# Attention over eight images: low-part products in groups of eight steps, V and q/k in other places

## The chip, the cores and the metric

The program runs on one core of a Trainium2 chip. The metric is the device time in microseconds of one execution. The engines are PE (TensorE, matmuls), DVE (VectorE), ACT (ScalarE), POOL (GpSimd) and SP (SyncE, which here only issues transfers). All times below are in microseconds unless marked otherwise.

## The reference

Self-attention over 8 images with 128 channels and 1024 pixels, with 64 channels for q and k; softmax runs over the second pixel index, and the result is scaled by gamma and added to the input.

```python
q = jnp.einsum('oc,bcn->bon', Wq, xf) + bq[None, :, None]
k = jnp.einsum('oc,bcn->bon', Wk, xf) + bk[None, :, None]
v = jnp.einsum('oc,bcn->bon', Wv, xf) + bv[None, :, None]
attn = jnp.einsum('bci,bcj->bij', q, k)
attn = jax.nn.softmax(attn, axis=-1)
out = jnp.einsum('bcn,bmn->bcm', v, attn).reshape(b, c, h, w)
return gamma * out + x
```

## The kernel before

An image is worked in two chunks of 512 pixels i (the queries), a chunk in 8 steps of 128 pixels j (the keys): 16 steps for an image, 128 in all. fp32 products are made from rounded high parts and low parts. The work of step s is a loop over s on each engine, written out by hand; semaphores couple them, and nothing but this order and the semaphores decides when something runs.

What PE does in step s, in this order:

- `score_tile(s + 2)` (L537, L538): the scores of the step after next, transposed, into one of two banks. It waits until ACT has read the bank two steps before (`weight_hi_done`).
- `max_jobs(s)` (L495, "mx" below): from step 18 on one product of 128 queries with 512 keys into a bank of `work`, from which DVE takes the row maximum (L768) that the softmax of a later chunk subtracts. In the first 18 steps a table, `EARLY_MAXES`, says how many, up to two.
- `sums_hi(s - 2)` (L556): four matmuls of 258 columns that add the high parts of the weights times the values to `sums`. Those of a chunk's first step wait, at the first and the third matmul, until DVE has read the sums of the chunk before (`sums_freed`).
- every `BURST` steps `sums_lo` (L572), the burst: the bf16 low parts of the weights of those steps times `values_b`. Of 16 matmuls (4 steps by 4 tiles) before. It goes through the first half of the tiles and then the second; after a chunk's last step each half releases `sums_done`.
- `side_jobs(s)`: with k the step in the image, V's product (L489, eight fp32 passes) in k = 1 and 9, the transposed output (L505) in k = 6 and 14, q and k together of the image after next (L482 to L484) in k = 7 and 11.

The mx products and the side jobs share the two banks of `work` in turn: job n takes the bank of job n - 2 and waits in `take_bank` until that has been read out. q/k is read out by ACT (`qk_hi`, L671) and then DVE (`qk_lo`, L759), V by ACT (L682) and then DVE (L764), an mx by DVE alone.

ACT makes, for the scores two steps ahead, two exponentials (L704 fp32 `weight`, L707 rounded `weight_hi`), then copies the low sums after a chunk's last step (`take_low_sum`, L713), then the side job, and in k = 3 and 5 the rounded input `x_hi` (L678). DVE makes in iteration s the side job of step s - 1, the maxima of step s, in steps k = 4, 8, 13, 15 and 0 of the weights their low part (`weight_lo`, L809, one iteration ahead), and behind a chunk's last step the total (L817) and its reciprocal. POOL makes the other low parts (L419), the scaled output (L426) in k = 3 and 11, `x_lo` (L400) in k = 4 and 6, and `values_b` (`short_values`, L411) in k = 2 and 10. `weight`, `weight_hi` and `weight_lo` are rings of 8 steps.

Of the kernel before, what the change touches and what calls it, by code (L numbers as in the profile page):

```python
# [5 lines left out]
BATCHES = 8  # L6
CHANNELS = 128
HEAD = 64
PIXELS = 32 * 32
TILE = 128  # L10
CHUNK = 512
# [8 lines left out]
VCOLS = 2 * CHANNELS + 2  # L20
# [3 lines left out]
RING = 8  # L24
# [12 lines left out]
ALL_ON_POOL = 8  # L37


BURST = 4  # L40

SPREAD_MX, SPREAD_REST = 4, 2

EARLY = 18
EARLY_MAXES = {5: (2, 0, 1), 6: (2, 1, 2), 7: (2, 3, 1), 8: (2, 4, 2), 9: (2, 6, 1), 10: (2, 7, 1),
               11: (3, 0, 1), 12: (3, 1, 2), 13: (3, 3, 1), 14: (3, 4, 1), 15: (3, 5, 1), 16: (3, 6, 1), 17: (3, 7, 1)}


def max_jobs(s):
# [3 lines left out]
    if s < EARLY:  # L55
        c, first, count = EARLY_MAXES.get(s, (0, 0, 0))
        return [(c, i) for i in range(first, first + count)]
# [4 lines left out]
def side_jobs(s):  # L62

    b, k = divmod(s, STEPS)
    jobs = []
    if k == 1 and b > 0:
        jobs.append(("v", b, 1))
    if b == 0 and k == 4:
        jobs.append(("mt", 1, 0))
    if k == 6 and b > 0:  # L70
        jobs.append(("out", 2 * b - 1, 0))
    if k in (7, 11) and b + 2 < BATCHES:
        jobs.append(("qk", b + 2, (7, 11).index(k)))
    if k == 9 and b + 1 < BATCHES:
        jobs.append(("v", b + 1, 0))
    if k == 14:
        jobs.append(("out", 2 * b, 0))
    return jobs


# [15 lines left out]
def low_on_dve(s):  # L96
    return s >= ALL_ON_POOL and s % STEPS in DVE_LOW
# [16 lines left out]
def loads(n, each=1):  # L114
    return 16 * each * ((n + 1) // 2 if n % 2 else n // 2)
# [7 lines left out]
def attention_program(nc, x, Wq, bq, Wk, bk, Wv, bv, gamma, out):  # L123
    fp32 = mybir.dt.float32
    fp32r = mybir.dt.float32r
    bf16 = mybir.dt.bfloat16
    ALU = mybir.AluOpType
# [6 lines left out]
    with ExitStack() as ctx:  # L134
        def sbuf(name, shape, dtype):
            return ctx.enter_context(nc.sbuf_tensor(name, shape, dtype))

        def psum(name, shape, dtype):
            return ctx.enter_context(nc.psum_tensor(name, shape, dtype))

        def sem(name):
            return ctx.enter_context(nc.semaphore(name))
# [34 lines left out]

        weight = sbuf("weight", [TILE, RING, CHUNK], fp32)
        weight_hi = sbuf("weight_hi", [TILE, RING, CHUNK], fp32r)
        weight_lo = sbuf("weight_lo", [TILE, RING, CHUNK], bf16)  # L180

        low_sum = sbuf("low_sum", [TILE, CHUNK_TILES, CHANNELS + 1], fp32)
        total = sbuf("total", [TILE, CHUNK_TILES, CHANNELS + 1], fp32)
# [5 lines left out]
        sums = psum("sums", [TILE, CHUNK_TILES, CHUNK], fp32)  # L189
# [18 lines left out]
        weight_lo_pool_done = sem("weight_lo_pool_done")  # L208
# [34 lines left out]
        weight_lo_done = sem("weight_lo_done")  # L243
# [13 lines left out]
        def tile(t):  # L257
            return slice(t * TILE, (t + 1) * TILE)
# [10 lines left out]
        def quarter(half):  # L269
            return slice(half * CHUNK_TILES, (half + 1) * CHUNK_TILES)  # L270
# [23 lines left out]
        def wait_lo_summed(engine, s):  # L294

            if s >= 0 and s % TILES >= TILES - BURST:
                engine.wait_ge(sums_done, 2 * (s // TILES + 1))
            elif s >= 0:
                engine.wait_ge(burst_done, s // TILES + 1)
# [66 lines left out]
        def _(pool):  # L366
# [42 lines left out]
            def short_values(n, half):  # L409
                pool.wait_ge(v_hi_done, HALVES * n + half + 1)  # L410
                pool.tensor_scalar(values_b[n % 2][:, quarter(half), 0:CHANNELS],  # L411
                                   values[n % 2][:, quarter(half), CHANNELS:2 * CHANNELS].bitcast(fp32), 0.0, 1.0,
                                   ALU.add, ALU.mult).then_inc(values_b_done, 1)

            def low_weights(s):
                pool.wait_ge(weight_hi_done, s + 1)
                wait_lo_summed(pool, s - RING)
                r = s % RING
                pool.tensor_tensor(weight_lo[:, r], weight[:, r], weight_hi[:, r], ALU.subtract).then_inc(weight_lo_pool_done, 1)  # L419

            def scale(c):
                pool.wait_ge(one_over_done, c + 1)

                wait(pool, out_turned, c)
                by = one_over[:, :].rearrange("p (t a) -> p t a", a=1).broadcast_to([TILE, CHUNK_TILES, CHANNELS])
                pool.tensor_tensor(scaled[:, :], total[:, :, 0:CHANNELS], by, ALU.mult).then_inc(scaled_done, 1)  # L426
# [10 lines left out]
            for s in range(ALL_STEPS):  # L437
                b, k = divmod(s, STEPS)
                if s + 1 < ALL_STEPS and not low_on_dve(s + 1):
                    low_weights(s + 1)  # L440
                if k == 3 and b > 0:
                    scale(2 * b - 1)
                if k == 11:
                    scale(2 * b)
                if k == 2 and b > 0:
                    short_values(b, 1)
                if k in (4, 6) and b + 2 < BATCHES:
                    rest_of_x(b + 2, (4, 6).index(k))
                if k == 10 and b + 1 < BATCHES:
                    short_values(b + 1, 0)  # L450

        @block.tensor
        def _(pe):
# [54 lines left out]
            def do_max(c, i):  # L508
                n, h = divmod(c, HALVES)
                if n > 0 and h == 0 and i == 0:  # L510
                    pe.wait_ge(spread_mx[n % 2], loads(n, SPREAD_MX))
                max_scores(n, h * CHUNK_TILES + i // 2, i % 2, take_bank(("mx", c, i)))

            def do_job(job):
                name, n, i = job
                place = take_bank(job)
                if name == "qk":
                    project_qk(n, i, place)
                elif name == "v":
                    wait_x(pe, n)  # L520
                    project_v(n, i, place)
                elif name == "mt":
                    pe.wait_ge(neg_max_r_done, n + 1)
                    turn_max(n, place)
                elif name == "out":
                    pe.wait_ge(scaled_done, n + 1)
                    turn_out(range(CHUNK_TILES), place)
# [32 lines left out]
            def sums_lo(s):  # L560

                b, k = divmod(s, STEPS)
                h, p = k // TILES, b % 2
                steps = range(s - BURST + 1, s + 1)
                if h == 0:
                    pe.wait_ge(values_b_done, HALVES * b + (k % TILES) // CHUNK_TILES + 1)
                for i in steps:
                    wait_low(pe, i)

                def lo(it, i):  # L570
                    j = i % TILES
                    return pe.matmul(sums[:, it, CHANNELS:VCOLS], weight_lo[:, i % RING, tile(it)],  # L572
                                     values_b[p][:, j], start=False, stop=(j == TILES - 1))

                for half in range(2):
                    for it in tiles_of_half(half):
                        for i in steps:
                            last = lo(it, i)
                    if s % TILES == TILES - 1:
                        last.then_inc(sums_done, 1)  # L580
                    elif half == 1:
                        last.then_inc(burst_done, 1)
# [50 lines left out]
            for s in range(ALL_STEPS + LAG):  # L633
                if s + AHEAD < ALL_STEPS:
                    score_tile(s + AHEAD)
                if s < ALL_STEPS:
                    for c, i in max_jobs(s):
                        do_max(c, i)
                if s >= LAG:
                    if s == LAG:  # L640

                        pe.wait_ge(qk_lo_done, HALVES)
                        pe.wait_ge(max_rows_done, 1)
                    sums_hi(s - LAG)
                    if (s - LAG) % BURST == BURST - 1:
                        sums_lo(s - LAG)
                if s < ALL_STEPS:
                    for job in side_jobs(s):
                        do_job(job)

            for half in range(2):
                pe.wait_ge(last_scaled, half + 1)
# [103 lines left out]
        def _(dve):  # L756
# [39 lines left out]
            def do_job(job):  # L796
                name, n, i = job
                if name == "qk":
                    rest_of_qk(n, i, bank(bank_of(job)))
                elif name == "v":  # L800
                    rest_of_v(n, i, bank(bank_of(job)))
                elif name == "out":
                    finish(n, bank(bank_of(job)))

            def low_weights(s):
                r = s % RING
                dve.wait_ge(weight_hi_done, s + 1)
                wait_lo_summed(dve, s - RING)
                dve.tensor_tensor(weight_lo[:, r], weight[:, r], weight_hi[:, r], ALU.subtract).then_inc(weight_lo_done, 1)  # L809

            def add_half(c, half):
                its = tiles_slice(half)
# [46 lines left out]
            for s in range(ALL_STEPS):  # L859
                b, k = divmod(s, STEPS)  # L860
# [55 lines left out]
```

## Time and profile before

| what | us |
|---|---|
| median of 3 runs | 240.57 |
| lowest and highest | 240.35, 241.44 |
| the profiled execution | 241.74 |
| its span in the trace | 239.7 |
| PE busy | 229.3 (96%) |
| ACT busy | 179.6 (75%) |
| POOL busy | 174.6 (73%) |
| DVE busy | 169.5 (71%) |

The profile records every instruction on each engine. A matmul is drawn until its modelled end, which overlaps the next one's start; so what PE's work takes is read from start to start. A timeline row merges instructions of one group that follow each other; its first two numbers are the start and the length, and a bracket at its end gives the idle time before it and the engine that ended it.

### The profile page before, as it was taken

What the parts mean: (1) busy time and instruction counts of PE and PEld (TensorE: products, weight loads), DVE (VectorE), ACT (ScalarE), POOL (GpSimd) and SP (SyncE); (2) the same over time, 40 slices, a digit from 0 to 9 for tenths busy, and PEclk for the clock granted to TensorE, in tenths of its full rate; (3) what the DMA queues carried; (4) which work ended last, traced back from release to release, by engine and by line L of the source; (5) the groups of instructions that cost most, each with busy time, mean ns of one, the idle gap of its engine ahead of it and who ended that gap; (6) DMA issues with size and microseconds to landing.
All of it is one profiled execution on the core that took longest, in us unless ns stands there. A gap on an engine that the chain in (4) does not pass through costs nothing.

```text
span 239.7 us, 4848 instructions
## 1 busy us (share of the span) xinstructions
PE 229.3 (96%) x1676; PEld 196.8 (82%) x1676; DVE 169.5 (71%) x287; ACT 179.6 (75%) x345; POOL 174.6 (73%) x158
## 2 busy tenths in 40 slices
PE   7997989899999999999999999999999999999992
PEld 7364968798889988898888898898888899899890
DVE  1486396776869768786869768787769767683354
ACT  2769768579786878779876887788776868778840
POOL 8568996279963898568972898658982977679750
PEclk9999999999999999999999999999999999999996
DMA  3714700490408403390407504291106601010101
GB/s 91 230 51 103 162 0 1 80 229 6 131 0 198 111 26 110 69 236 4 131 4 177 131 3 133 40 233 38 44 3 151 158 0 45 4 44 3 44 37 51
DMA packets 16103, 19.86 MB, mean 83 GB/s; under 512 B 9808, under 2 KB 10320, under 8 KB 16080
## 3 DMA queue, kind: packets, MB, share of 16 engines
q1 hardware_dynamic: 15840, 19.54, 33.0%
q8 instruction: 13, 0.21, 0.4%
q14 instruction: 10, 0.08, 0.1%
q10 hardware_dynamic: 240, 0.03, 0.1%
HBM read 4.33 MB, written 4.19 MB: 36 GB/s over the span
## 4 chain that ended last, share of the span: by engine, by line
PE 92%; DVE 3%; ACT 3%; issue 1%; POOL 0%; POOLq 0%; DVEq 0%
PE sums L556 25%; PE sums L572 13%; PE scores L537 12%; PE work L495 12%; PE scores L538 12%; PE work L489 6%; PE work L505 3%; PE sums L586 2%; PE work L483 1%; PE work L484 1%; PE work L482 1%; DVE neg_max L768 1%; DVE qk_lo L759 1%; PE scores L489 1%; PE sums L478 1%
## 5 line engine op out<-in xcount | busy, mean ns | idle before, releaser
L419 POOL TENSOR_TENSOR weight_lo<-weight,weight_hi 128x512 bf16<-128x512 f32 x90 | 122.5, 1381 | 43.6 <-ACT weight_hi L707 43.4
L768 DVE TENSOR_REDUCE neg_max<-work 128x1 f32<-128x512 f32 x120 | 81.8, 686 | 22.9 <-PE work L495 22.4
L704 ACT ACTIVATE weight<-scores 128x512 f32<-128x512 f32 x128 | 76.9, 600 | 27.5 <-PE scores L538 24.7
L556 PEld LDWEIGHTS sums<-values,weight_hi 128*128 128x128 f32 x512 | 78.1, 188 | 10.2 <-issue 0.5
L556 PE MATMUL sums<-values,weight_hi 128*128 128x258 f32 x512 | 81.7, 282 | 0.1
L707 ACT ACTIVATE weight_hi<-scores 128x512 fp32r<-128x512 f32 x128 | 76.9, 600 | 0.0
L537 PE MATMUL scores<-q_hihi,k_hilo 128*128 128x512 f32 x128 | 54.5, 426 | 1.1 <-ACT weight_hi L707 1.1
L495 PE MATMUL work<-k_hilo,q_hihi 128*128 128x512 f32 x120 | 48.9, 413 | 2.4 <-DVE qk_lo L759 2.0
L538 PE MATMUL scores<-q_lomax,k_hione 128*128 128x512 f32 x128 | 50.4, 393 | 0.0
L809 DVE TENSOR_TENSOR weight_lo<-weight,weight_hi 128x512 bf16<-128x512 f32 x38 | 36.5, 961 | 2.7 <-ACT weight_hi L707 2.7
L572 PE MATMUL sums<-values_b,weight_lo 128*128 128x130 bf16 x512 | 35.5, 221 | 0.0
L495 PEld LDWEIGHTS work<-k_hilo,q_hihi 128*128 128x128 f32 x120 | 22.4, 188 | 14.5 <-DVE qk_lo L759 6.5
L572 PEld LDWEIGHTS sums<-values_b,weight_lo 128*128 128x128 bf16 x512 | 29.8, 98 | 1.5
L537 PEld LDWEIGHTS scores<-q_hihi,k_hilo 128*128 128x128 f32 x128 | 24.2, 189 | 3.2 <-ACT weight_hi L707 1.9
L538 PEld LDWEIGHTS scores<-q_lomax,k_hione 128*128 128x128 f32 x128 | 24.3, 190 | 0.6
L817 DVE TENSOR_TENSOR total<-sums,low_sum 128x258 f32<-128x258 f32 x32 | 13.6, 427 | 11.7 <-ACT low_sum L713 11.1
L713 ACT ACTIVATE low_sum<-sums 128x256 f32<-128x256 f32 x32 | 12.4, 386 | 6.9 <-PE sums L572 4.7
L426 POOL TENSOR_TENSOR scaled<-total,one_over 128x512 f32<-128x512 f32 x15 | 15.6, 1042 | 0.0
L489 PE MATMUL work<-w_v_t,x_sb 128*128 128x128 f32 x112 | 15.5, 281 | 0.0
L400 POOL TENSOR_TENSOR x_lo<-x_sb,x_hi 128x512 fp32r<-128x512 f32 x12 | 15.4, 1284 | 0.0
L411 POOL TENSOR_SCALAR values_b<-values 128x512 bf16<-128x512 f32 x16 | 9.9, 617 | 7.1 <-ACT values L682 7.1
L764 DVE TENSOR_TENSOR values<-work,values 128x512 fp32r<-128x512 f32 x14 | 9.7, 692 | 7.3 <-ACT values L682 7.3
(78 smaller groups left out, 167.6 us busy)
## 6 DMA issues: line engine op xcount, KB each, us to landing
out<-y_sb SPq DMA_DIRECT2D x15, 256.0 KB, 2.4
x_sb<-in_x SPq DMA_DIRECT2D x7, 512.0 KB, 4.0
q_hihi<-qk_hi SPq DMA_DIRECT2D x14, 256.0 KB, 3.8
k_hilo<-qk_hi SPq DMA_DIRECT2D x7, 256.0 KB, 3.1
k_hilo<-qk_lo SPq DMA_DIRECT2D x7, 256.0 KB, 4.9
q_lomax<-qk_lo SPq DMA_DIRECT2D x7, 256.0 KB, 5.0
k_hione<-qk_hi SPq DMA_DIRECT2D x7, 256.0 KB, 4.9
q_lomax<-neg_max_r SPq DMA_DIRECT2D x56, 0.5 KB, 2.1
```

Source lines behind the costliest of these rows:

```text
L419: pool.tensor_tensor(weight_lo[:, r], weight[:, r], weight_hi[:, r], ALU.subtract).then_inc(weight_lo_pool_done, 1)
L426: pool.tensor_tensor(scaled[:, :], total[:, :, 0:CHANNELS], by, ALU.mult).then_inc(scaled_done, 1)
L489: last = pe.matmul(place[:, tile(t)], image(n)[:, tile(half * CHUNK_TILES + t)], w_v_t[:, :], start=True, stop=True)
L495: pe.matmul(place, q_hihi[p][:, tile(t)], k_hilo[p][:, chunk(h)], start=True, stop=True).then_inc(mx_done, 1)
L537: pe.matmul(scores[:, s % 2], k_hilo[p][:, tile(j)], q_hihi[p][:, chunk(h)], start=True, stop=False)
L538: pe.matmul(scores[:, s % 2], k_hione[p][:, tile(j)], q_lomax[p][:, chunk(h)], start=False, stop=True).then_inc(scores_done, 1)
L556: last = pe.matmul(sums[:, it, 0:VCOLS], weight_hi[:, r, tile(it)], values[p][:, j], start=(j == 0), stop=False)
L572: return pe.matmul(sums[:, it, CHANNELS:VCOLS], weight_lo[:, i % RING, tile(it)], values_b[p][:, j], start=False, stop=(j == TILES - 1))
L704: act.activation(weight[:, r], scores[:, s % 2], ACT.Exp)
L707: act.activation(weight_hi[:, r], scores[:, s % 2], ACT.Exp).then_inc(weight_hi_done, 1)
L768: dve.reduce_max(neg_max[:, t, h:h + 1], place, AX.X, negate=True).then_inc(neg_max_done, 1)
L809: dve.tensor_tensor(weight_lo[:, r], weight[:, r], weight_hi[:, r], ALU.subtract).then_inc(weight_lo_done, 1)
```

## The change

- `BURST` is 8 instead of 4: a burst holds 32 matmuls (8 steps by 4 tiles) and comes once for each chunk, in k = 1 and k = 9, no more in k = 5 and 13. `weight_lo` becomes a ring of 16 steps (`LOW_RING`).
- V's two halves are made in k = 15 of the image before and in k = 3, not in k = 9 of the image before and k = 1. On POOL `short_values` moves to k = 0 and k = 4.
- q/k is made in k = 8 and 12, and on PE ahead of `sums_hi` of that step; the other side jobs stay behind it.
- Four entries of `EARLY_MAXES` change, so that the steps of the first image with a q/k product hold one mx, and steps 7 and 11 hold two.

```diff
-BURST = 4
+BURST = 8
+LOW_RING = 16
...
-EARLY_MAXES = {5: (2, 0, 1), 6: (2, 1, 2), 7: (2, 3, 1), 8: (2, 4, 2), 9: (2, 6, 1), 10: (2, 7, 1),
+EARLY_MAXES = {5: (2, 0, 1), 6: (2, 1, 2), 7: (2, 3, 2), 8: (2, 5, 1), 9: (2, 6, 1), 10: (2, 7, 1),
...
-    if k == 1 and b > 0:
+    if k == 3 and b > 0:
         jobs.append(("v", b, 1))
...
-    if k in (7, 11) and b + 2 < BATCHES:
-        jobs.append(("qk", b + 2, (7, 11).index(k)))
-    if k == 9 and b + 1 < BATCHES:
-        jobs.append(("v", b + 1, 0))
+    if k in (8, 12) and b + 2 < BATCHES:
+        jobs.append(("qk", b + 2, (8, 12).index(k)))
     if k == 14:
         jobs.append(("out", 2 * b, 0))
+    if k == 15 and b + 1 < BATCHES:
+        jobs.append(("v", b + 1, 0))
...
-                wait_lo_summed(pool, s - RING)
+                wait_lo_summed(pool, s - LOW_RING)
...
-                if k == 2 and b > 0:
+                if k == 0 and b > 0:
+                    short_values(b, 0)
+                if k == 4 and b > 0:
                     short_values(b, 1)
                 if k in (4, 6) and b + 2 < BATCHES:
                     rest_of_x(b + 2, (4, 6).index(k))
-                if k == 10 and b + 1 < BATCHES:
-                    short_values(b + 1, 0)
...
+                    for job in side_jobs(s):
+                        if job[0] == "qk":
+                            do_job(job)
                 if s >= LAG:
...
                     for job in side_jobs(s):
-                        do_job(job)
+                        if job[0] != "qk":
+                            do_job(job)
```

On PE, around the end of an image (step k = 1 of the next one): the sums and the burst that end a chunk, and what follows up to the first sums of the new chunk. Before:

```order
L556 MATMUL sums<-values1,weight_hi 128x258 x4
L572 MATMUL sums<-values_b1,weight_lo 128x130 x16
L489 MATMUL work<-w_v_t,x_sb 128x128 x4
L537 MATMUL scores<-q_hihi0,k_hilo0 128x512
L538 MATMUL scores<-q_lomax0,k_hione0 128x512
L495 MATMUL work<-k_hilo1,q_hihi1 128x512
L556 MATMUL sums<-values0,weight_hi 128x258 x4
```

And of the change:

```order
L557 MATMUL sums<-values1,weight_hi 128x258 x4
L573 MATMUL sums<-values_b1,weight_lo 128x130 x32
L538 MATMUL scores<-q_hihi0,k_hilo0 128x512
L539 MATMUL scores<-q_lomax0,k_hione0 128x512
L496 MATMUL work<-k_hilo1,q_hihi1 128x512
L557 MATMUL sums<-values0,weight_hi 128x258 x4
```

The burst is twice as long, and V's product no longer stands between it and the new chunk's sums.

On DVE, around steps 7 to 9 of an image: the output's last addition, the maxima, a low part of the weights and the low part of q/k. Before:

```order
L786 SCALAR_TENSOR_TENSOR y_sb<-work,gamma_bv,x_sb 128x512
L768 TENSOR_REDUCE neg_max<-work 128x1
L809 TENSOR_TENSOR weight_lo<-weight,weight_hi 128x512
L759 SCALAR_TENSOR_TENSOR qk_lo<-work,b_qk,qk_hi 128x512
L768 TENSOR_REDUCE neg_max<-work 128x1 x2
```

And of the change:

```order
L791 SCALAR_TENSOR_TENSOR y_sb<-work,gamma_bv,x_sb 128x512
L773 TENSOR_REDUCE neg_max<-work 128x1
L814 TENSOR_TENSOR weight_lo<-weight,weight_hi 128x512
L773 TENSOR_REDUCE neg_max<-work 128x1
L764 SCALAR_TENSOR_TENSOR qk_lo<-work,b_qk,qk_hi 128x512
L773 TENSOR_REDUCE neg_max<-work 128x1
```

A maximum stands directly behind the low part now, with qk_lo one place later.

On POOL, in steps 4 to 8 of an image: low parts of the weights and the two x_lo. Before:

```order
L419 TENSOR_TENSOR weight_lo<-weight,weight_hi 128x512
L400 TENSOR_TENSOR x_lo<-x_sb,x_hi 128x512
L419 TENSOR_TENSOR weight_lo<-weight,weight_hi 128x512 x2
L400 TENSOR_TENSOR x_lo<-x_sb,x_hi 128x512
L419 TENSOR_TENSOR weight_lo<-weight,weight_hi 128x512 x3
```

And of the change:

```order
L420 TENSOR_TENSOR weight_lo<-weight,weight_hi 128x512
L412 TENSOR_SCALAR values_b<-values 128x4x128
L401 TENSOR_TENSOR x_lo<-x_sb,x_hi 128x512
L420 TENSOR_TENSOR weight_lo<-weight,weight_hi 128x512 x2
L401 TENSOR_TENSOR x_lo<-x_sb,x_hi 128x512
```

values_b stands in this chain now, ahead of the first x_lo.

## Rows read from the trace of the kernel before

**Rows 1.** Windows: busy time of each engine (instructions), clock, DMA share, GB/s.

```profile
105.00:118.00 13.00, 13.00 (x102) 11.65 (x101) 9.50 (x17) 10.77 (x22) 12.24 (x11) 1.00 0.35 82
```

**Rows 2.** Timeline of PE, image 3, steps 1 to 6: start, length, group.

```profile
105.74 1.11 PE L572 MATMUL sums<-values_b,weight_lo 128*128 128x130 bf16 x16
106.69 1.11 PE L489 MATMUL work<-w_v_t,x_sb 128*128 128x128 f32 x8
107.55 0.48 PE L537 MATMUL scores<-q_hihi,k_hilo 128*128 128x512 f32 x1
107.86 0.40 PE L538 MATMUL scores<-q_lomax,k_hione 128*128 128x512 f32 x1
...
108.80 0.40 PE L537 MATMUL scores<-q_hihi,k_hilo 128*128 128x512 f32 x1
...
112.35 1.11 PE L572 MATMUL sums<-values_b,weight_lo 128*128 128x130 bf16 x16
113.27 0.48 PE L537 MATMUL scores<-q_hihi,k_hilo 128*128 128x512 f32 x1
```

**Rows 3.** Timeline of PE in the opening: V without a burst before it.

```profile
14.35 1.05 PE L489 MATMUL scores<-w_v_t,x_sb 128*128 128x128 f32 x8
15.16 0.71 PE L495 MATMUL work<-k_hilo,q_hihi 128*128 128x512 f32 x2
```

**Rows 4.** Timeline of PE, image 3, step 9.

```profile
118.24 0.39 PE L538 MATMUL scores<-q_lomax,k_hione 128*128 128x512 f32 x1
118.55 0.50 PE L495 MATMUL work<-k_hilo,q_hihi 128*128 128x512 f32 x1
118.89 0.65 PE L556 MATMUL sums<-values,weight_hi 128*128 128x258 f32 x4
```

**Rows 5.** PE in image 0: a wait of step 12 in the timeline; both waits summed.

```profile
43.00 0.50 PE L495 MATMUL work<-k_hilo,q_hihi 128*128 128x512 f32 x1 [0.89 <-DVE qk_lo L759]
43.34 0.63 PE L556 MATMUL sums<-values,weight_hi 128*128 128x258 f32 x4
...
PE work L495 <- DVE qk_lo L759: 2.0, 2, 1.2
```

**Rows 6.** Timeline of ACT and DVE behind the burst of 105.74.

```profile
106.42 0.85 ACT L713 ACTIVATE low_sum<-sums 128x256 f32<-128x256 f32 x2
106.83 0.90 DVE L817 TENSOR_TENSOR total<-sums,low_sum 128x258 f32<-128x258 f32 x2 [0.49 <-ACT low_sum L713]
```

**Rows 7.** Timeline of PE in the last image, behind the burst of step 9.

```profile
225.37 0.40 PE L538 MATMUL scores<-q_lomax,k_hione 128*128 128x512 f32 x1
...
225.88 0.80 PE L556 MATMUL sums<-values,weight_hi 128*128 128x258 f32 x4
```

**Rows 8.** Timeline of ACT in image 3, V and the exponential behind it.

```profile
107.83 0.60 ACT L682 ACTIVATE values<-work 128x512 fp32r<-128x512 f32 x1 [0.56 <-PE work L489]
108.33 0.59 ACT L704 ACTIVATE weight<-scores 128x512 f32<-128x512 f32 x1
```

**Rows 9.** Timeline of DVE and POOL, image 3, steps 2 to 8, and the tail.

```profile
108.52 0.62 POOL L411 TENSOR_SCALAR values_b<-values 128x512 bf16<-128x512 f32 x1 [0.27 <-ACT values L682]
...
110.63 1.56 POOL L419 TENSOR_TENSOR weight_lo<-weight,weight_hi 128x512 bf16<-128x512 f32 x1 [0.49 <-ACT weight_hi L707]
...
112.15 1.28 POOL L400 TENSOR_TENSOR x_lo<-x_sb,x_hi 128x512 fp32r<-128x512 f32 x1
...
113.37 2.56 POOL L419 TENSOR_TENSOR weight_lo<-weight,weight_hi 128x512 bf16<-128x512 f32 x2
...
115.87 1.32 POOL L400 TENSOR_TENSOR x_lo<-x_sb,x_hi 128x512 fp32r<-128x512 f32 x1
...
116.47 1.27 DVE L809 TENSOR_TENSOR weight_lo<-weight,weight_hi 128x512 bf16<-128x512 f32 x1
...
228.21 1.04 POOL L426 TENSOR_TENSOR scaled<-total,one_over 128x512 f32<-128x512 f32 x1
...
228.31 1.48 DVE L809 TENSOR_TENSOR weight_lo<-weight,weight_hi 128x512 bf16<-128x512 f32 x1 [1.98 <-ACT weight_hi L707]
```

More of the change, by code:

```diff
@@ L37 @@
 ALL_ON_POOL = 8
-BURST = 4
+BURST = 8
+LOW_RING = 16
 SPREAD_MX, SPREAD_REST = 4, 2
 EARLY = 18
-EARLY_MAXES = {5: (2, 0, 1), 6: (2, 1, 2), 7: (2, 3, 1), 8: (2, 4, 2), 9: (2, 6, 1), 10: (2, 7, 1),
-               11: (3, 0, 1), 12: (3, 1, 2), 13: (3, 3, 1), 14: (3, 4, 1), 15: (3, 5, 1), 16: (3, 6, 1), 17: (3, 7, 1)}
+EARLY_MAXES = {5: (2, 0, 1), 6: (2, 1, 2), 7: (2, 3, 2), 8: (2, 5, 1), 9: (2, 6, 1), 10: (2, 7, 1),
+               11: (3, 0, 2), 12: (3, 2, 1), 13: (3, 3, 1), 14: (3, 4, 1), 15: (3, 5, 1), 16: (3, 6, 1), 17: (3, 7, 1)}
 def max_jobs(s):
@@ L179, in attention_program @@
         weight_hi = sbuf("weight_hi", [TILE, RING, CHUNK], fp32r)
-        weight_lo = sbuf("weight_lo", [TILE, RING, CHUNK], bf16)
+        weight_lo = sbuf("weight_lo", [TILE, LOW_RING, CHUNK], bf16)
         low_sum = sbuf("low_sum", [TILE, CHUNK_TILES, CHANNELS + 1], fp32)
@@ L416, in low_weights @@
                 pool.wait_ge(weight_hi_done, s + 1)
-                wait_lo_summed(pool, s - RING)
+                wait_lo_summed(pool, s - LOW_RING)
                 r = s % RING
-                pool.tensor_tensor(weight_lo[:, r], weight[:, r], weight_hi[:, r], ALU.subtract).then_inc(weight_lo_pool_done, 1)
+                pool.tensor_tensor(weight_lo[:, s % LOW_RING], weight[:, r], weight_hi[:, r], ALU.subtract).then_inc(weight_lo_pool_done, 1)
             def scale(c):
@@ L571, in lo @@
                     j = i % TILES
-                    return pe.matmul(sums[:, it, CHANNELS:VCOLS], weight_lo[:, i % RING, tile(it)],
+                    return pe.matmul(sums[:, it, CHANNELS:VCOLS], weight_lo[:, i % LOW_RING, tile(it)],
                                      values_b[p][:, j], start=False, stop=(j == TILES - 1))
@@ L807, in low_weights @@
                 dve.wait_ge(weight_hi_done, s + 1)
-                wait_lo_summed(dve, s - RING)
-                dve.tensor_tensor(weight_lo[:, r], weight[:, r], weight_hi[:, r], ALU.subtract).then_inc(weight_lo_done, 1)
+                wait_lo_summed(dve, s - LOW_RING)
+                dve.tensor_tensor(weight_lo[:, s % LOW_RING], weight[:, r], weight_hi[:, r], ALU.subtract).then_inc(weight_lo_done, 1)
             def add_half(c, half):
```

## The prediction

> **What bounds the kernel now.** I read a thirteen-microsecond window of the steady part first: TensorE (PE) is busy all of it, DVE 9.5, ACT 10.8 and POOL 12.2, at a granted clock of 1.00, the 2.4 GHz level [rows 1]. So a microsecond counts only where PE loses it, and busy time does not say where that is, because a matmul that waits for its weights is drawn longer. I therefore read the distances between the starts of PE's groups. In a step without extras, scores take 0.23 + 0.23, the maxima's product (L495, "mx") 0.235 and the four sums 0.48: 1.18. I call Tn the start of the scores issued in step n of an image, so T2 is 107.55 and T3 108.80 [rows 2]; image b has steps 0 to 15, and PE never stands still except where a distance exceeds these. Two kinds of losses are visible: waits for a bank of `work` behind q and k, and a longer first score after every other kind of matmul. The profiled run is 241.74 for a span of 239.7; the median shown is 240.57. I sum changes of the span and add them to the median.
>
> **1. Waits behind q and k: gone, gain 4.0.** The mx two jobs after a q/k product needs its bank, and gets it after ACT's qk_hi and DVE's qk_lo. In step 9 this makes two distances 0.31 and 0.34 instead of 0.235 [rows 4]: 0.2 lost, the same in step 13, in images 1 to 5: 5 × 0.4 = 2.0. In image 0, whose steps 8 and 12 hold two mx, the waits are 1.16 and 0.89 [rows 5]; counted by starts 0.26 more each (a matmul drawn 0.39 long against a distance of 0.235, and 0.10 for the late weights): 1.4 + 1.15 = 2.6. In the new order q and k stand ahead of the sums, 0.48 earlier before that mx, and the q/k of step 8 also has the burst of 32 behind it. It asks for the bank 0.48 later where it asked 0.2 too early, so this wait goes with 0.28 to spare, if ACT and DVE are as prompt. In image 0 DVE now meets five mx in steps 5 to 7 without the burst between: at 0.69 each against two mx per 1.4, I let it give back 0.3 in step 7 and 0.3 in step 12. Net 2.0 + 2.6 − 0.6 = 4.0.
>
> **2. Fewer switches: gain 0.7.** A burst of 16 alone takes 0.92 and its first score afterwards 0.31 instead of 0.23; burst and V together 0.95 + 0.86 + the same 0.08 [rows 2]. The change halves the bursts, but takes V away from them, so that V pays a return of its own: six returns per image before and six after. What is left: V alone took 0.81 in the opening instead of 0.86 [rows 3], and a burst of 32 should take 0.01 + 32 × 0.0589 − 0.03 = 1.87 (0.0589 is what 16 pitches make of 0.95, less the first's 0.01). Per image 2 × (0.99 + 1.89) = 5.76 becomes 2 × (1.95 + 0.89) = 5.68. Eight images: 0.7. Were all halved bursts worth a return, it would be 2 × 0.08 × 8 = 1.3; the least is zero.
>
> **3. The end of each chunk loses its cover: loss 3.3.** This is the term that the diff doesn't show. Before a new chunk's sums may overwrite `sums`, ACT copies the low sum and DVE adds, by halves (`sums_freed`). In the old burst this is over 1.99 after its start (106.83 + 0.90 = 107.73, burst at 105.74), that is 1.10 after its last matmul began [rows 6]. V, 0.86 on PE, lay over it. Now the last of 32 begins 1.84 into the burst; the second half is free at 2.94, PE hears of it at 3.00. PE, with no V, reaches the third of the next sums' matmuls at 1.87 + 0.31 + 2 × 0.235 + 2 × 0.118 = 2.89. A matmul whose weights come late begins some 0.105 after that load (43.00 to 43.34, where 0.235 is the rule [rows 5]), so it starts at 3.11: 0.22 lost. The old trace has one chunk end without V, in the last image, also without mx: there 538 takes 0.51 instead of 0.23, and the four sums are drawn 0.80 long instead of 0.64, a loss of 0.28 + 0.16 = 0.44 [rows 7]; with an mx of 0.235 ahead, 0.21 is what the sum gives. Thirteen chunk ends in images 0 to 6 at 0.22 are 2.9; that of step 1 in the last image has no mx and costs 0.45; that of step 9 there is unchanged. 3.3. The least it can be is 0 (if I mistake the order of readers), the most 15 × 0.44 = 6.6.
>
> **4. V in step 3 delays ACT: loss 0.3.** ACT starts V 0.03 after V's matmuls end (107.83 [rows 8], V drawn from 106.69 for 1.11 [rows 2]), so at T3 + 2.27, and follows with x_hi, both ahead of the exponentials of step 6's weights. Operations of 0.6 follow each other there after 0.50 [rows 8]: with V, x_hi and the first exponential at 0.5 each and the second at 0.6, ACT is done at T3 + 4.37, and score 8 wants it at T3 + 4.47. With 0.06 for the signal and 0.105 for late weights, 0.06 is lost in images 1 to 5. Zero to 0.15 each.
>
> **5. DVE's low part of step 8 against POOL's second x_lo: loss 3.3, or nothing.** DVE and POOL hold each other up here: DVE's weight_lo takes 0.68 alone, but 1.27 when issued at 116.47 into POOL's x_lo of 115.87, and 1.48 at 228.31, one tenth behind POOL's product of 228.21 [rows 9]. The reverse is seen too: POOL's weight_lo of 110.63 takes 1.56 instead of 1.28. Before, the q/k of step 7 and not step 8's mx was next on DVE, and nothing of PE waited. Now mx 9 takes the bank of mx 8, and DVE reads mx 8 right behind this weight_lo. When does it start? POOL begins weight_lo 5 at T3 + 1.83 (110.63 − 108.80); 1.47 later short_values (now here; 0.62 drawn, 0.58 counted), x_lo (112.15 to 113.37: 1.23), two low parts (113.37 to 115.87: 2.50) and then the second x_lo at T3 + 7.61. DVE's low part stands at T7 + 1.6, as before. T7 is T3 + 1.18 + 0.81 (V) + 1.26 + 1.22 + 0.06 (4.) + 1.53 (step 6 with out) = T3 + 6.06; DVE is there at T3 + 7.66, five hundredths behind POOL. If that counts as behind, the low part ends 0.6 after x_lo, at T3 + 9.5; mx 8 is read at 10.2, and mx 9, due on PE at T9 + 0.47 = T3 + 9.67, starts at 10.34: 0.67 lost, in each of images 1 to 5: 3.3. The bounds are 0 and, with image 0, 4.0. I take the loss: rows at one tenth behind show the block in full, and anything more that delays PE between steps 3 and 7 keeps DVE behind for up to another 1.2, while POOL's chain has little to delay it.
> The Trainium skill has a rule on this ("SBUF — State Buffer", section "SBUF: two separate sides"): a DVE operation with two SBUF inputs and a GpSimd operation that reads SBUF exclude each other, and whichever starts first has the port pair for its whole instruction. By that rule the sum is the one with the loss; without it, it would be 3.3 less. The trace agrees with full blocking (1.48 for 0.68), and has no row within five hundredths.
>
> **What costs nothing.** The ring of 16 removes no wait, since waits on freed low parts don't show in the trace. DVE's part of V in step 15 ends just under 0.1 before mx needs the bank, as after V now. The next image's spread is issued about as late as before, because it also waits for the last scores. In the tail both orders do the same matmuls after the last exponential: −0.1, with 0.1 lost in the last image's steps without mx, where PE no longer leaves ACT a burst to catch up.
>
> **Sum.** −4.0 − 0.7 + 3.3 + 0.3 + 3.3 = +2.2 to 2.4 (2.35 before rounding): 240.57 + 2.35 = **242.9**.
>
> **Rivals.** (A) DVE gets ahead of POOL in step 7. For it: five hundredths is within the error of a sum of nine distances. Then 3.35 is not lost: −1.0, 239.6 (238.8 to 240.6). (B) The forecast, slower: 242.9 (242 to 244); it decides from the point at which DVE's low part starts after x_lo. (C) The cover of 3. isn't needed, because ACT or DVE is faster behind a longer burst than behind a short one, and A holds too: −1.0 − 3.0 gives 236.6. Against it stands the last image's row. (D) The race is lost a second time: DVE's low part of the next step 0 starts 0.08 ahead of POOL's (it does so now); behind it, V's rest on DVE ends at T1 + 1.1 instead of 0.35, and the mx of step 1, due at 0.47, waits some 0.65 in seven images: 242.9 + 4.5 = 247.4. (E) Some images block and some don't: 240 to 242.
>
> **How the numbers follow.** B 0.45, A 0.27, C 0.10, D 0.08, E 0.10. The range 238.8 to 244.2 leaves out C, D and a rim of A. A measurement tells about 0.5% from no change, that is 239.4 to 241.8. Faster: C and 0.12 of A, 0.22. The same: the rest of A and most of E, 0.25. Slower: B, D, a little E: 0.53. B's own range is 242.0 to 244.2.
>
> **What would show it.** The sums of steps 2 and 10 at 0.70 instead of 0.48 (3.); 538 and mx of steps 10 and 14 at 0.235 (1.); V at 0.81 and the burst at 1.87 (2.); a weight_lo of 1.8 on DVE in step 7 or 8 and an mx of step 9 that waits for neg_max (5.; in A it is 0.68 and no wait); score 8 waiting for weight_hi (4.). The prediction is wrong if the sums behind a burst of 32 don't wait, or if DVE slips in ahead of x_lo.

## The result, and the profile after

The changed kernel takes 245.2 us (median of 4, 244.6 to 245.5) beside 240.8 for the kernel before: 1.018 times as long, 95% interval 1.015 to 1.021, which is 4.3 us more (3.5 to 5.0). The forecast was 242.9, with 244.2 as the upper end.

PE's busy share and clock say nothing of this. The page and the same window as in [rows 1]:

```profile
PE 232.1 (96%) x1676; PEld 197.9 (82%) x1676; DVE 166.2 (68%) x287; ACT 180.2 (74%) x345; POOL 175.5 (72%) x158
...
PE 84%; DVE 9%; ACT 4%; issue 2%; POOL 0%; POOLq 0%; DVEq 0%
...
105.00:118.00 13.00, 12.85 (x96) 11.03 (x93) 9.43 (x16) 10.57 (x22) 10.87 (x10) 1.00 0.32 84
```

The second line is the chain that ended last. In the kernel before it was PE for 92% and DVE for 3%; now DVE holds 9% of it. The waits, summed over the whole span of the changed kernel (engine, operation, who ended the wait: us, times, longest; PEld is PE's loading of weights), name the places:

```profile
PEld work L496 <- DVE neg_max L773: 5.9, 10, 0.7
PEld sums L557 <- DVE total L822: 2.8, 15, 0.4
PEld work L490 <- DVE y_sb L791: 1.2, 7, 0.2
```

None of the three is in the list of before, except a neg_max wait of 1.4 in all; the wait for qk_lo, 6.5 in all there, is gone. What they are in the steady part is read from PE's starts, as before. Image 3 of the changed kernel, the chunk end of step 1 (timeline):

```profile
104.69 2.04 PE L573 MATMUL sums<-values_b,weight_lo 128*128 128x130 bf16 x32
105.83 0.39 ACT L718 ACTIVATE low_sum<-sums 128x256 f32<-128x256 f32 x1 [0.62 <-PE sums L573]
106.25 0.43 DVE L822 TENSOR_TENSOR total<-sums,low_sum 128x258 f32<-128x258 f32 x1 [0.96 <-ACT low_sum L718]
106.53 0.48 PE L538 MATMUL scores<-q_hihi,k_hilo 128*128 128x512 f32 x1
106.76 0.38 ACT L718 ACTIVATE low_sum<-sums 128x256 f32<-128x256 f32 x1 [0.55 <-PE sums L573]
107.18 0.43 DVE L822 TENSOR_TENSOR total<-sums,low_sum 128x258 f32<-128x258 f32 x1 [0.50 <-ACT low_sum L718]
107.32 0.85 PE L557 MATMUL sums<-values,weight_hi 128*128 128x258 f32 x4
...
108.01 0.39 PE L538 MATMUL scores<-q_hihi,k_hilo 128*128 128x512 f32 x1
```

The four sums take 0.69 (107.32 to 108.01) instead of 0.48: the second half's total ends at 107.61, 2.92 after the burst began, and their third matmul waits for it. In [rows 6] the same two additions were over 1.99 after the burst, with V still on PE.

Steps 8 and 9 of the same image:

```profile
115.64 1.30 POOL L401 TENSOR_TENSOR x_lo<-x_sb,x_hi 128x512 fp32r<-128x512 f32 x1
115.68 1.80 DVE L814 TENSOR_TENSOR weight_lo<-weight,weight_hi 128x512 bf16<-128x512 f32 x1
...
117.41 0.68 DVE L773 TENSOR_REDUCE neg_max<-work 128x1 f32<-128x512 f32 x1
117.45 0.40 PE L539 MATMUL scores<-q_lomax,k_hione 128*128 128x512 f32 x1
...
118.14 0.50 PE L496 MATMUL work<-k_hilo,q_hihi 128*128 128x512 f32 x1 [0.30 <-DVE neg_max L773]
118.49 0.64 PE L557 MATMUL sums<-values,weight_hi 128*128 128x258 f32 x4
```

DVE's low part starts 0.04 after POOL's x_lo (0.07 in the next image) and takes 1.80 instead of 0.68. The maximum behind it, which reads the bank that the mx of step 9 takes, is over at 118.09, and that mx, whose two distances were 0.31 and 0.34 in [rows 4], has 0.69 and 0.35: 0.57 lost against 0.235 twice.

Behind q and k the mx of step 10 comes without a wait, and the sums behind it wait as those of step 2 do:

```profile
121.13 0.40 PE L539 MATMUL scores<-q_lomax,k_hione 128*128 128x512 f32 x1
121.37 0.40 PE L496 MATMUL work<-k_hilo,q_hihi 128*128 128x512 f32 x1
121.60 0.85 PE L557 MATMUL sums<-values,weight_hi 128*128 128x258 f32 x4
122.29 0.39 PE L538 MATMUL scores<-q_hihi,k_hilo 128*128 128x512 f32 x1
```

Step 15, V behind the output:

```profile
128.62 0.75 DVE L791 SCALAR_TENSOR_TENSOR y_sb<-work,gamma_bv,x_sb 128x512 f32<-128x512 f32 x1
128.82 0.63 PE L557 MATMUL sums<-values,weight_hi 128*128 128x258 f32 x4
...
129.42 1.16 PE L490 MATMUL work<-w_v_t,x_sb 128*128 128x128 f32 x8
...
130.34 0.48 PE L538 MATMUL scores<-q_hihi,k_hilo 128*128 128x512 f32 x1
```

V is due 0.48 after the sums and starts after 0.60, then takes 0.92 instead of the 0.81 of [rows 3]: 0.22 lost, because its bank holds the output, which DVE adds up until 129.37.

Most useful is the length of an image, from the start of the scores issued in step 0 to the same place of the next, since the opening ahead of it differs by up to 1.3 us between these profiles (that start stands at 19.7 in the profile of before and 18.7 in that of the change). From the timelines:

| kernel | image 0 | each of images 1 to 5 | image 6 |
|---|---|---|---|
| before | 29.10 | 27.3 | 25.50 |
| the change | 27.23 | 28.13 | 26.08 |
| e1_xlo_later | 27.69 | 27.58 | 26.11 |
| e8_v_in_step_0 | (30.22) | 27.84 | 25.83 |
| e7_pool_nudge | (33.35) | 27.57 | 26.09 |
| e6_second_v_back | 27.24 | 27.61 | 25.87 |
| e10_both_waits | 26.67 | 27.30 | 25.80 |
| e3_qk_only | 27.16 | 26.93 | 25.54 |
| e4_burst_only | 28.46 | 27.97 | 25.38 |
| e2_v_back | 27.33 | 26.79 | 25.40 |
| e9_v_back_short_start | 26.50 | 26.79 | 25.40 |

With bursts of 32, image 0 holds 16 low matmuls fewer (0.95) and the last image as many more. The two values in brackets are of executions with a long wait in image 0 that comes and goes (its rows stand in the last section); the ratios leave out the long executions: two of the four of e7_pool_nudge (247.8, 248.5) and one each of e8_v_in_step_0 (246.5), e5_v_back_short_ends (240.6) and e6_second_v_back (245.8, not profiled). Between the change and before, images 0 to 6 differ by −1.87 + 4.13 + 0.58, and the rest of the span, from step 0 of the last image, by 30.02 − 28.90 = 1.12: 3.96 together. The whole spans differ by 3.0 only, because the profiled execution of before had the longer opening.

### The profile page after: what moved, and what is told of

It is laid out like the page before. It is cut to its first block, busy times and chain, and to the rows that moved or that the text cites. A ratio compares the mean times of both kernels' runs of the same rounds, so it can differ in the third digit from the quotient of the medians.

```text
span 242.7 us, 4840 instructions
## 1 busy us (share of the span) xinstructions
PE 232.1 (96%) x1676; PEld 197.9 (82%) x1676; DVE 166.2 (68%) x287; ACT 180.2 (74%) x345; POOL 175.5 (72%) x158
## 4 chain that ended last, share of the span: by engine, by line
PE 84%; DVE 9%; ACT 4%; issue 2%; POOL 0%; POOLq 0%; DVEq 0%
PE sums L557 24%; PE sums L573 12%; PE work L496 11%; PE scores L538 11%; PE scores L539 10%; PE work L490 6%; DVE weight_lo L814 4%; PE work L506 3%; DVE neg_max L773 2%; PE sums L587 2%; DVE y_sb L791 1%; PE scores L490 1%; PE work L483 1%; PE sums L479 1%; ACT weight L709 1%
## 5 line engine op out<-in xcount | busy, mean ns | idle before, releaser
L420 POOL TENSOR_TENSOR weight_lo<-weight,weight_hi 128x512 bf16<-128x512 f32 x90 | 124.1, 1397 | 45.3 <-ACT weight_hi L712 45.3
L557 PEld LDWEIGHTS sums<-values,weight_hi 128*128 128x128 f32 x512 | 79.1, 188 | 12.8 <-DVE total L822 2.8
L557 PE MATMUL sums<-values,weight_hi 128*128 128x258 f32 x512 | 84.6, 285 | 0.4 <-DVE total L822 0.4
L496 PE MATMUL work<-k_hilo,q_hihi 128*128 128x512 f32 x120 | 48.3, 409 | 1.9 <-DVE neg_max L773 1.8
L814 DVE TENSOR_TENSOR weight_lo<-weight,weight_hi 128x512 bf16<-128x512 f32 x38 | 34.0, 894 | 3.0 <-ACT weight_hi L712 3.0
L573 PE MATMUL sums<-values_b,weight_lo 128*128 128x130 bf16 x512 | 32.7, 220 | 0.0
L687 ACT ACTIVATE values<-work 128x512 fp32r<-128x512 f32 x14 | 8.4, 600 | 8.6 <-PE work L490 8.6
```

What stands on the lines that cost most here:

```text
L420: pool.tensor_tensor(weight_lo[:, s % LOW_RING], weight[:, r], weight_hi[:, r], ALU.subtract).then_inc(weight_lo_pool_done, 1)
L496: pe.matmul(place, q_hihi[p][:, tile(t)], k_hilo[p][:, chunk(h)], start=True, stop=True).then_inc(mx_done, 1)
L557: last = pe.matmul(sums[:, it, 0:VCOLS], weight_hi[:, r, tile(it)], values[p][:, j], start=(j == 0), stop=False)
L814: dve.tensor_tensor(weight_lo[:, s % LOW_RING], weight[:, r], weight_hi[:, r], ALU.subtract).then_inc(weight_lo_done, 1)
```

## The experiments

### The port: e1_xlo_later

```diff
-                if k in (4, 6) and b + 2 < BATCHES:
-                    rest_of_x(b + 2, (4, 6).index(k))
+                if k in (4, 8) and b + 2 < BATCHES:
+                    rest_of_x(b + 2, (4, 8).index(k))
```

> The changed kernel with one number changed: POOL makes the second x_lo of an image in its iteration 8 instead of 6, so that it doesn't stand in the way of DVE's low part of step 8. Theory of the port race: the low part takes 0.7 instead of 1.80, the mx of step 9 comes without a wait (538 at 0.23 instead of 0.69), 0.57 less in each of images 1 to 5, 2.9 in all: some 242.3 us beside 245.2. Rival (mx 9 waits because qk_hi and qk_lo come late, whatever POOL does): no change, 245.

242.25 us, 1.007 times the kernel before (1.0045 to 1.009), where the change has 1.018: 2.6 us came back by the ratios, 2.9 were expected. An image takes 27.58 instead of 28.13; image 0 is 0.46 longer in this profile, where DVE's low part of its step 8 takes 1.83 instead of 1.36. DVE's low part in its timeline, and PE's step 9:

```profile
116.12 0.68 DVE L814 TENSOR_TENSOR weight_lo<-weight,weight_hi 128x512 bf16<-128x512 f32 x1
...
117.89 0.40 PE L539 MATMUL scores<-q_lomax,k_hione 128*128 128x512 f32 x1
118.12 0.40 PE L496 MATMUL work<-k_hilo,q_hihi 128*128 128x512 f32 x1
```

0.68 and 0.23: no wait. q/k is where it was, so the rival on qk_lo falls.

### The port again, by added work: e7_pool_nudge

```diff
+                if k == 5 and b + 2 < BATCHES:
+                    pool.memset(scratch[:, :], 0.0)
```

(`scratch` is a new tile that nothing else uses.)

> The changed kernel with one operation more: POOL sets 128x128 elements of an unused tile to zero in its iteration 5, some 0.2 us, so that its second x_lo starts some 0.15 behind DVE's low part of step 8 instead of 0.04 before it (115.64 and 115.68 in the changed kernel). Theory of the port race: the added work makes the kernel faster, the low part takes 0.7, the mx of step 9 comes without a wait, 5 times 0.57 less: 242.4 us beside 245.2. Rival (POOL's load as such, or qk_lo, delays step 9): unchanged or slower, 245.2 to 246.2.

1.010 times the kernel before (1.007 to 1.013), some 242.9 us, where the change has 1.018. An image takes 27.57, as in e1_xlo_later. The added 0.2 us on POOL reverses who starts first:

```profile
148.00 0.69 DVE L817 TENSOR_TENSOR weight_lo<-weight,weight_hi 128x512 bf16<-128x512 f32 x1
148.10 1.75 POOL L402 TENSOR_TENSOR x_lo<-x_sb,x_hi 128x512 fp32r<-128x512 f32 x1
```

Now POOL's x_lo is the one held up (1.75 for 1.3), and nobody waits for that. The rule of the Trainium skill ("SBUF — State Buffer", section "SBUF: two separate sides"), that whichever of the two starts first keeps the port for its whole instruction, agrees with these traces down to a lead of 0.04 us one way (the change) and 0.10 the other (here).

### V behind the bursts again: e2_v_back

```diff
-    if k == 3 and b > 0:
+    if k == 1 and b > 0:
         jobs.append(("v", b, 1))
...
-    if k == 15 and b + 1 < BATCHES:
+    if k == 9 and b + 1 < BATCHES:
         jobs.append(("v", b + 1, 0))
```

(with POOL's `short_values` back in k = 2 and 10)

> The changed kernel with V's halves (and POOL's short_values) back where they were before: behind the bursts of steps 9 and 1. Theory: V covers the reading of the sums again, so the sums behind a chunk's end take 0.48 instead of 0.69 (13 times 0.22 and once 0.45, 3.3 us), the wait of V in step 15 for the bank of the output goes (7 times 0.22, 1.5 us), and POOL's second x_lo starts earlier than DVE's low part needs the way, which takes the 2.9 us of step 9 as well: some 238 us. Rival (the longer burst of 32 costs by itself, by starving ACT and DVE): V's place gives back 3.3 at most, 242 us.

237.3 us, 0.986 times the kernel before (0.983 to 0.988), 7.9 us less than the change. Its chunk end in step 1:

```profile
103.85 1.11 PE L490 MATMUL work<-w_v_t,x_sb 128*128 128x128 f32 x8
104.71 0.48 PE L538 MATMUL scores<-q_hihi,k_hilo 128*128 128x512 f32 x1
...
105.50 0.64 PE L557 MATMUL sums<-values,weight_hi 128*128 128x258 f32 x4
105.98 0.39 PE L538 MATMUL scores<-q_hihi,k_hilo 128*128 128x512 f32 x1
```

The sums take 0.48 behind the same burst of 32. So its length is not what makes them wait; V's place is. In this kernel DVE's low part of step 8 takes 1.01, and step 9 has no wait. What the long burst is worth in total is told behind e4_burst_only.

### One half of V back: e6_second_v_back

```diff
-    if k == 3 and b > 0:
+    if k == 1 and b > 0:
         jobs.append(("v", b, 1))
```

> The changed kernel with only V's second half back behind the burst of step 1; the first half stays in step 15. Theory of the lost cover: the sums of step 2 take 0.48 again, those of step 10 still 0.69; 6 times 0.22 and once 0.45, 1.8 us. PE is also 0.9 earlier in step 7 while POOL's chain stays, so DVE's low part falls into POOL's low part before x_lo and waits less, and most of the 2.9 us of step 9 goes too: 241 us. Rival (the sums behind a burst wait because of its length, not because V is missing): step 2 stays at 0.69, and only the race changes: 242.5 us.

241.6 us, 1.0045 times the kernel before (1.002 to 1.007). The two chunk ends of one image separate the theories: in image 4 the sums of step 2 go from 134.72 to 135.20, 0.48, those of step 10 from 147.59 to 148.28, 0.69. But only 0.2 of step 9's 0.57 went, not most of it: DVE's low part, at 141.86, falls into POOL's low part ahead of x_lo and still takes 1.62. An image is 0.52 shorter: 0.22 at the chunk end, 0.2 in step 9, 0.12 for steps 5 and 6, where ACT no longer makes V and x_hi in a row, less 0.04 for V's own reading.

### V's first half in step 0: e8_v_in_step_0

```diff
+    if k == 0 and b > 0:
+        jobs.append(("v", b, 0))
...
-    if k == 15 and b + 1 < BATCHES:
-        jobs.append(("v", b + 1, 0))
```

> The changed kernel with V's first half in step 0 of its own image instead of step 15 of the one before. Theory: in step 15 V waits for the bank of the transposed output of step 14, which DVE reads late (7 times 0.22); in step 0 the bank is free, and the burst of step 1 covers V's reading (0.05 less too). The port race is left as it is. 245.2 - 1.9 = 243.3 us. Rival (V waits wherever it stands after the output, since DVE is behind): unchanged, 245.

1.013 times the kernel before (1.010 to 1.017): 1.1 us less than the change, of the 1.9 expected; the intervals allow both. The images are clearer: 27.84 instead of 28.13, 0.29 each, with V starting 0.48 behind the sums and taking 0.81:

```profile
133.12 0.64 PE L557 MATMUL sums<-values,weight_hi 128*128 128x258 f32 x4
133.60 1.05 PE L490 MATMUL work<-w_v_t,x_sb 128*128 128x128 f32 x8
134.41 0.47 PE L538 MATMUL scores<-q_hihi,k_hilo 128*128 128x512 f32 x1
```

### Both waits away: e10_both_waits

The edits of e1_xlo_later and e8_v_in_step_0 together.

> The changed kernel with the edits of e1_xlo_later (second x_lo in POOL's iteration 8) and e8_v_in_step_0 (V's first half in step 0) together; bursts of 32 and V's second half in step 3 stay. Theory: the two waits are independent, an image of the steady part goes from 28.13 to 28.13 - 0.55 - 0.29 = 27.29 us, that of the kernel before; what q/k gained is then just eaten by the sums behind the bursts. 245.2 - 2.9 - 1.9 = 240.4 us. Rival (they share a cause, DVE being behind): 242.

241.0 us, 1.001 times the kernel before (0.998 to 1.004). An image takes 27.30: the two add up, and what the move of q/k gained is eaten by the chunk ends.

### Only the move of q and k: e3_qk_only

The kernel before with `(8, 12)` for q/k, ahead of the sums, and the new `EARLY_MAXES`.

> The kernel before with only the move of q and k (steps 8 and 12, ahead of the sums) and the table of the first image's maxima; bursts of 16 and V as before. Theory: the waits for qk_lo in steps 9 and 13 go (2.0 us in images 1 to 5, 2.6 in image 0), given back by about 0.1 per image in step 9 and 0.5 to 1 in image 0: some 237.5 us. Rival (the mx that follows meets DVE's low part of step 8 held up by POOL, as in the changed kernel): 0.57 per image back, 240 us.

237.0 us, 0.984 (0.982 to 0.987). Images 1 to 5 take 26.93 instead of 27.3, image 0 27.16 instead of 29.10. This part of the change is worth nearly 4 us by itself. Its DVE low part of step 8 is held up as well (1.22 at 113.14), but not long enough to reach the mx of step 9.

### Only the long bursts: e4_burst_only

The kernel before with `BURST = 8` and the ring of 16; V behind the bursts, q/k in steps 7 and 11.

> The kernel before with only the bursts of 32 and the ring of 16 low parts. Theory: two round trips between kinds of matmul fewer per image at 0.06 each (0.9 us in all), V still covers the chunk's end, and image 0 loses some 0.5 where the burst of step 5 hid ACT: 240.3 us beside 240.8. Rival (the burst of 32 itself is at fault for part of the loss): slower than 241.5.

244.5 us, 1.015 (1.0115 to 1.018): the theory was wrong by 4 us, and the rival had the direction (slower than 241.5) but not the reason. The burst as such costs nothing (it takes 1.88 before V, and the sums behind it 0.48). The loss sits in step 14:

```profile
127.78 1.29 POOL L420 TENSOR_TENSOR weight_lo<-weight,weight_hi 128x512 bf16<-128x512 f32 x1 [0.87 <-ACT weight_hi L708]
128.03 1.60 DVE L810 TENSOR_TENSOR weight_lo<-weight,weight_hi 128x512 bf16<-128x512 f32 x1
...
129.08 0.63 PE L557 MATMUL sums<-values,weight_hi 128*128 128x258 f32 x4
129.55 1.28 DVE L769 TENSOR_REDUCE neg_max<-work 128x1 f32<-128x512 f32 x2
130.28 0.66 PE L506 MATMUL work<-identity,scaled 128*128 128x128 f32 x4 [0.57 <-DVE neg_max L769]
```

The same collision stands in the kernel before (POOL's low part at 126.30, DVE's at 126.55 for 1.58). There the burst of step 13 follows on PE, and the output of step 14 starts 0.48 behind its sums (128.59 and 129.07), without a wait. Here that burst is gone, the output needs the bank of the mx of step 13, and it waits 0.72. With q/k moved as well (e2_v_back), qk_lo no longer stands ahead of this low part: DVE starts it at 122.09, 0.33 ahead of POOL's of 122.42, it takes 0.81, and an image takes 26.79 instead of 27.97.

But even with the move the long burst does not pay in these runs. Against e3_qk_only an image of the steady part is 0.14 shorter; from step 0 of image 0 to the end e2_v_back takes 216.2 and e3_qk_only 216.0, because the last image is 0.90 longer and image 0, which should be as much shorter by the matmuls moved out of it, is 0.17 longer. The medians, 237.3 and 237.0, cannot tell the two apart.

### Short bursts at the ends: e5, e9; step 8 on POOL: e11

```diff
+SHORT_BURSTS = (0, 15)
...
+def burst_of(s):
+    if s // TILES in SHORT_BURSTS:
+        return BURST // 2 if s % (BURST // 2) == BURST // 2 - 1 else 0
+    return BURST if s % BURST == BURST - 1 else 0
```

> The changed kernel with V back behind the bursts (as in e2_v_back, 237.3 us), and bursts of 16 in the first chunk (steps 3 and 7 of the first image) and in the last chunk. Theory: in the first image the burst of step 5 again lies over PE's wait for ACT (0.56), in the tail the shorter last burst lets the last half be added up 0.6 earlier: 236.1 us. Rival (both are hidden by other waits): 237.3.

> The changed kernel with V back behind the bursts, and bursts of 16 in the first chunk only (e5 without the short ones of the last chunk). Theory: the burst of step 5 of the first image lies over 0.56 of waiting for ACT, and the last burst of 32 costs nothing over two of 16, since one return less pays for the later end: 236.7 us beside 237.3 for e2_v_back. Rival (the first image is bound by DVE and POOL anyway): 237.3.

With `(0, 15)` 237.0 us (0.985, 0.982 to 0.9875), with `(0,)` 237.0 (0.988, 0.982 to 0.994): neither can be told from e2_v_back. In the profile of the second, image 0 is 0.83 shorter than in e2_v_back: 0.56 of that is the wait for ACT in step 5, as expected, and most of the rest is in step 9, where DVE's low part takes 1.06 instead of 1.35. The last image is the same. In whole executions this doesn't show beside an opening that varies by more.

> e2_v_back (237.3 us) with the low part of step 8 of the first image on POOL instead of DVE (ALL_ON_POOL 9). In that image POOL works without a gap, and DVE's low part there took 1.35 us in e2_v_back, 3.57 to 5.20 in three other profiles. Theory: it waits through one or more of POOL's operations; without it the first image is 0.2 to 0.3 shorter: 237.0 us, and no execution is longer by some microseconds. Rival (POOL's extra 1.3 us delays the burst of step 9): 238.

237.0 us (0.985, 0.981 to 0.989); image 0 takes 27.14 instead of 27.33, the 0.2 expected, and again no difference to be measured. Whether it does away with the long waits of the last section is not shown, since the four executions of e2_v_back had none either. All of e2, e3, e5, e9 and e11 beat both kernels, at 237.0 to 237.3.

## Why the prediction was right or wrong

The direction was right and the size too small: +2.35 against +4.3, and the upper end of the range missed by 1.0. Two steps failed. "What costs nothing" put V in step 15 at nothing, and it waits 0.22 in each of seven images (1.5 us) for a bank that DVE has not read out. Term 1 let image 0 give back 0.3 + 0.3 to DVE's maxima, and image 0 gave back 1.0 more, over half of it to a wait for ACT. Point by point:

**1, q and k (−4.0).** Right as a mechanism and in the steady part: the mx of steps 10 and 14 comes at 0.23, and e3_qk_only shows 0.37 per image and 1.94 in image 0. In the changed kernel image 0 kept less. It is 1.87 shorter, of which 0.95 is the matmuls moved out of it, so 0.9 where the terms gave about 1.9. The step that failed is the sentence that gave the early steps 0.3 + 0.3. It looked at DVE's maxima, which did cost about that or less (0.24 in step 7 and 0.12 in step 12). But the first to be late without the burst of step 5 was ACT: the scores issued in step 6 are the first of a chunk and need the row of maxima that ACT writes. They start 1.04 after the sums of step 5 instead of 0.48, when that row is done (27.00 + 0.58):

```profile
26.60 0.64 PE L557 MATMUL sums<-values,weight_hi 128*128 128x258 f32 x4
27.00 0.58 ACT L693 ACTIVATE q_lomax<-work 1x512 fp32r<-1x512 f32 x1
...
27.64 0.50 PE L538 MATMUL scores<-q_hihi,k_hilo 128*128 128x512 f32 x1 [0.41 <-ACT q_lomax L693]
```

With the burst of step 5 back, in e9_v_back_short_start, they start 1.39 after the sums with 0.92 of burst between, so the wait is covered. The rest of image 0's shortfall is V in step 15 (0.22) and step 9 (0.25).

**2, switches (−0.7).** Its pieces were right: V took 0.81 in step 3 and the burst 1.85. The case that the prediction gives as the most, where V stays behind the bursts and each halved burst saves a return (0.16 per image), is that of e2_v_back against e3_qk_only, and they differ by 0.14.

**3, the lost cover (+3.3).** Right to the hundredth, and worked out ahead: the second half was free 2.92 after the burst began (2.94 forecast), the sums take 0.69 at each of the chunk ends of images 0 to 6 (0.21 to 0.22 lost), and 0.45 in step 2 of the last image. e2_v_back and e6_second_v_back show that V's place is the cause and the length of the burst is not.

**4, ACT behind V in step 3 (+0.3).** The mechanism was right, the size 0.12 per image instead of 0.06: the sums of step 5 have 0.52 and score 8's first matmul 0.31. With V's second half out of step 3, in e6_second_v_back, they have 0.47 and 0.23. 0.3 us more.

**5, DVE and POOL (+3.3).** The case taken was the one that came: DVE 0.04 to 0.07 behind POOL, 0.05 forecast. The sum had POOL at T3 + 7.61 and DVE at T3 + 7.66, and image 3 of the trace has 7.63 and 7.67. But five hundredths are within the error of nine distances, as the prediction says itself (T7 came 0.04 later than the sum had it), so that it came out on this side is partly luck. The loss was 0.57 per image, not 0.67: 0.5 less. Two runs took it away in two ways, e1_xlo_later and e7_pool_nudge.

**What costs nothing.** Here the prediction failed most. It weighed V of step 15 only by who waits for its bank afterwards (that mx is 0.05 late, as it was behind V before: right), and not by whose bank it takes: that of the output, made in step 14 two jobs before, which DVE reads behind a maximum and a low part. 0.22 in seven images, 1.5 us; e8_v_in_step_0 gives it back. V in step 9 took the bank of an mx long read.

**The sum.** 2.35, and 1.3 for V in step 15 of images 1 to 6, 1.0 for image 0, 0.3 for ACT, less 0.5 for the port, is 4.4; measured are 4.3. That the two agree to a tenth is luck: the interval of the measured is 1.5 wide, and the lengths read from the two traces give 3.96. Of what lies between, 0.2 is the tail: behind the last scores it is 0.3 shorter, where 0.1 was forecast. The range was too narrow by what it left out altogether: each unit of moved work was given its known bounds, but no allowance was made for a wait that nobody had listed.

## What to carry to other kernels

When an operation moves, ask both questions of each shared buffer: who waits for it afterwards, and who held it before. Look at what the operation lay over in its old place, since the busy share of an engine that is always busy shows neither the cover nor its loss. And of a change in several parts, measure each alone: here moving q and k alone was worth 4 us, and moving V cost 8 beside it. The long burst alone cost 3.6 us, most of it in step 14, where nothing had been changed but the burst ahead of it.

## What the runs showed of the hardware

- Two operations of DVE and POOL that exclude each other make a kernel's time hang on 0.04 us: 0.2 us of added work on POOL took 0.55 us off each of five images (e7_pool_nudge against the change).
- DVE does not always get its turn when POOL's operation ends. In the first image POOL works without a gap, and one low part of DVE, 0.7 us of work, took 5.20 there: it was let in only when three more operations of POOL had ended, at 35.67. From the timeline of e7_pool_nudge:

```profile
30.69 1.29 POOL L402 TENSOR_TENSOR x_lo<-x_sb,x_hi 128x512 fp32r<-128x512 f32 x1
...
31.01 5.20 DVE L817 TENSOR_TENSOR weight_lo<-weight,weight_hi 128x512 bf16<-128x512 f32 x1
...
31.95 3.72 POOL L421 TENSOR_TENSOR weight_lo<-weight,weight_hi 128x512 bf16<-128x512 f32 x3
```

The same operation took 3.85 in the profile of e8_v_in_step_0 and 3.57 in that of e5_v_back_short_ends, where it was let in when two more had ended, and 1.06 to 1.83 in those where it was let in at the first end. PE stood idle for 3.80 behind it, and its clock was granted at 0.50 in the window from 36 to 40 of e7_pool_nudge, the 1.2 GHz level. What decides whether DVE is let in stays open.
